# A small vision network on one core: norms and routing at both ends of the attention heads are moved amid neighbouring work

## The chip, the core and the metric

The kernel runs on one NeuronCore of a Trainium2 chip. The time is the device time of one execution in microseconds (us). Five engines run side by side, each through its own list of instructions, and wait for one another by semaphores: TensorE (PE: matrix products, into the eight banks of PSUM), VectorE (DVE), ScalarE (ACT: functions by table), GpSimd (POOL) and SyncE (SP: it issues transfers). "PEld" is TensorE's loading of stationary operands.

## What is computed

Four images of 224 by 224 with 3 channels are cut into 784 patches each, of 8 by 8 pixels. The steps, with h as the running state (784 tokens of 64 features per image):

```python
h = tokenizer(x)                              # two layer norms, a projection, a silu layer
h = h + gated_group_norm(layernorm(h))        # the sequence mixer; its group norm has groups of one
h = h + experts0(layernorm(h))                # shared MLP + 4 experts of 3 layers, top 2 (relu)
h = h + attention(layernorm(h))               # 8 heads, rank 32: softmax(q k / 8) x VO
h = h + experts1(layernorm(h))                # softmax router, top 2 of 8 experts: gelu(x w1 + b1) w2 + b2
```

A layer norm here is the mean taken off, then a product with (variance + 1e-5)^-0.5. The output holds h three times per image. What matters for the change: the norm before the attention can be taken image by image, since it needs the first expert layer of that image alone; the norm and the router before the last expert layer need all 8 heads of that image alone.

## The kernel before

**Layout.** An image's 784 tokens lie in two halves of 392 columns: rows 0 to 63 of a tile hold the features of the first half, rows 64 to 127 those of the second. `H` is the state, `xhat` the normalised state. P is the PSUM, `bank(n)` is 392 columns of bank n.

**A norm** (`norm(S)`, one in each engine's list; S is `ATT` before the attention and `MOE1` before the last expert layer) has these steps for images 0 to 3 together: TensorE centres `H` by a product into a bank; ScalarE squares it; VectorE copies it to `xhat`; TensorE averages the squares of all images into one bank, 32 rows per image; ScalarE loads the table of Ln, takes Ln, loads the table of Exp and takes Exp(-0.5 times that); TensorE spreads the result over 128 rows per image; VectorE multiplies it into `xhat` (semaphore `normed`).

**The first expert layer** is a loop over images b in all lists: second layer, shared second layer, then the first layer of image b+1, the gates broadcast by products, and the sums into bank 7, which VectorE adds to `H` (L1382, semaphore `h_ready`). ScalarE empties the hidden banks 0 to 3 (L535). Afterwards comes `norm(ATT)` for all four images.

**Projections.** `project_pair(b, n)` makes half of the heads' q or k of image b (n counts `QK_ORDER`: q and k of heads 0 to 3, q and k of heads 4 to 7). Each has to be split in a high and a low part (`QKH`, `QKL`). For image 0 ScalarE writes the high part and VectorE the low one (L568, L1390); for the others ScalarE writes the raw value (`project_raw`, L577) and GpSimd splits it (L676, L678; `qk_split` counts). SyncE copies the parts of a head into the stacks `Qs` and `Ks` with six transfers (`fill_stacks`, L389), sends features for the values (`features_in`, L379), values (`fill_values`, L393 and L394) and the row of negative maxima (`rows_to_stack`, L400), in one queue in the order of its list. Before the heads comes the lead-in, a loop over `LEAD` = 14 steps j: two products (`max_half`) whose row maxima VectorE takes (L1395), for heads 0 and 1; in between, by the table `BETWEEN`, projections and the values (`turn_values`) of later images. In the kernel before image 0 and image 1 are projected ahead of the lead-in and images 2 and 3 within.

**Heads.** `four_heads(i)` runs 4 heads; 8 calls make 32 heads, the middle six in a loop. A head is 14 score products (`score_half`), each exponentiated by ScalarE (L610), beside them the row-max products of the head two ahead, and then its context (`context_tile`, seven pairs), which ScalarE copies (L618, `CT`) and TensorE projects in the next head (`head_out`); VectorE divides (`divide`), GpSimd adds (`add_head`). The last two heads have no head two ahead, and so no row-max products.

**The end.** Then `OUT` is turned back onto `H` for all images ("join"), `norm(MOE1)` follows, the router's logits are turned, VectorE finds top 2 and gates (`route`, some 18 small instructions), TensorE turns the gates to rows and VectorE copies them (`wT1`). 16 steps m (image m // 4, expert pair m % 4) follow: a hidden layer, Gelu (L642), a broadcast of the gates, VectorE's product of both (L1525) and the second layer's product. Twelve hidden layers run ahead of the first gates. The sum of an image is added (L1517), turned, copied by ScalarE (L656) and stored, 3 copies for each of two parts, 21 of the 24 stores by SyncE and the last 3 by ScalarE (L363).

## Time and profile before

| | us |
|---|---|
| median of 3 runs | 611.97 |
| lowest and highest | 611.2, 613.12 |
| the profiled execution | 613.25 |
| its span in the profile | 611.4 |
| TensorE busy | 563.2 (92%) |
| VectorE busy | 373.6 (61%) |
| ScalarE busy | 328.4 (54%) |
| GpSimd busy | 75.2 (12%) |

The profile is of one execution. Its time is longer than its span by what lies before the first and after the last instruction. Matmuls are pipelined, so a busy TensorE isn't TensorE at its peak. A product of 4-byte numbers is two matmul instructions in it, a product of operands rounded for speed ("fp32r") is one.

### The profile page before, as it was taken

To read this page: it belongs to the slowest core of one execution; us is meant where nothing else is said; L and a number is where in the kernel's file an instruction comes from. 1 tells how busy PE (TensorE), PEld (TensorE's weight loads), DVE (VectorE), ACT (ScalarE), POOL (GpSimd) and SP (SyncE) were. 2 spreads that over 40 slices of the span, in tenths; PEclk is the share of its full clock that TensorE was granted. 3 is DMA by queue.
4 is the path that set the end of the run, shared out by engine and by line. 5 is a ranking of instruction groups with operands and counts; after the bars stand their busy time and mean duration, and the time that the engine had idled before them with its cause. 6 is when DMAs were issued, how large, how long until landed. Compare 5 with 4: busy or idle time off the path is not lost.

```text
span 611.4 us, 10204 instructions
## 1 busy us (share of the span) xinstructions
PE 563.2 (92%) x3076; PEld 330.1 (54%) x3076; DVE 373.6 (61%) x881; ACT 328.4 (54%) x726; POOL 75.2 (12%) x89
## 2 busy tenths in 40 slices
PE   0689799997989999999999999999999999997994
PEld 0454344443556566566576576666666676452441
DVE  3844754214697667677677577577577677036562
ACT  0464758563746456466466465465465565536521
POOL 0000000000696100100100100100100001112000
PEclk9999999998989999999999999999999999999997
DMA  6500000000551322322322422323323320000015
GB/s 171 227 0 2 0 0 2 0 1 14 125 144 40 102 72 66 99 68 73 93 64 75 97 58 78 94 58 82 90 58 88 84 58 19 2 1 1 1 39 119
DMA packets 21986, 37.65 MB, mean 62 GB/s; under 512 B 5560, under 2 KB 15224, under 8 KB 21704
## 3 DMA queue, kind: packets, MB, share of 16 engines
q1 hardware_dynamic: 21606, 36.82, 23.3%
q10 hardware_dynamic: 354, 0.50, 0.4%
q8 instruction: 14, 0.23, 0.2%
q14 instruction: 12, 0.10, 0.1%
HBM read 6.07 MB, written 2.41 MB: 14 GB/s over the span
## 4 chain that ended last, share of the span: by engine, by line
PE 89%; ACT 4%; DVE 2%; DMA 2%; issue 1%; SPq 0%; DVEq 0%
PE P L702 86%; DMA X<-x 2%; PE P L718 2%; PE P L985 1%; ACT L504 1%; ACT PT L610 1%; ACT g L642 1%; DVE bst L1187 1%; PE P L1125 0%; DVE xhat L1259 0%; SPq L369 0%; ACT act L513 0%; PE P L844 0%; PE P L955 0%; DVE mx L1395 0%
## 5 line engine op out<-in xcount | busy, mean ns | idle before, releaser
L1395 DVE TENSOR_REDUCE mx<-P 112x1 f32<-112x392 f32 x448 | 219.0, 557 | 96.2 <-PE P L702 91.8
L610 ACT ACTIVATE PT<-P 112x392 f32<-112x392 f32 x448 | 188.2, 494 | 26.6 <-PE P L702 25.5
L702 PE MATMUL P<-Ks,Qs 96*112 96x392 f32 x448 | 167.8, 379 | 1.0 <-DVE mx L1395 0.9
L702 PE MATMUL P<-Qs,Ks 98*112 98x392 f32 x448 | 155.3, 351 | 0.8 <-ACT PT L610 0.7
L702 PE MATMUL P<-PT,XVs 112*64 112x392 f32 x896 | 154.5, 496 | 0.0
L702 PEld LDWEIGHTS P<-PT,XVs 112*64 112x64 f32 x896 | 61.6, 137 | 79.3 <-issue 73.6
L702 PEld LDWEIGHTS P<-Ks,Qs 96*112 96x112 f32 x448 | 78.8, 178 | 42.7 <-issue 19.7
L618 ACT ACTIVATE CT<-P 128x392 f32<-128x392 f32 x32 | 15.9, 497 | 134.4 <-PE P L702 134.4
L702 PEld LDWEIGHTS P<-Qs,Ks 98*112 98x112 f32 x448 | 79.9, 179 | 6.2 <-ACT PT L610 3.7
L688 POOL TENSOR_TENSOR OUT<-OUT,part 120x448 f32<-120x448 f32 x27 | 30.7, 1136 | 274.1 <-DVE part L1422 274.1
L702 PE MATMUL P<-VBs,CT 128*112 128x130 f32 (+1 forms) x320 | 40.0, 261 | 0.6 <-ACT CT L618 0.6
L702 PE MATMUL P<-xhat,wa 64*128 64x392 f32 (+2 forms) x144 | 37.8, 560 | 1.4 <-DVE xhat L1259 1.4
L702 PEld LDWEIGHTS P<-VBs,CT 128*112 128x112 f32 (+1 forms) x320 | 35.3, 157 | 6.0 <-ACT CT L618 1.3
L535 ACT ACTIVATE h<-P,wa 128x392 f32<-128x392 f32 x48 | 24.5, 596 | 13.9 <-PE P L702 13.8
L718 PE MATMUL P<-wa,xn 112*96 112x112 f32 x56 | 12.1, 398 | 16.2 <-DVE xn L1200 16.2
L702 PEld LDWEIGHTS P<-xhat,wa 64*128 64x128 f32 (+2 forms) x144 | 17.1, 192 | 17.5 <-DVE xhat L1259 4.2
L676 POOL CAST QKH<-QKL 128x392 fp32r<-128x392 f32 x24 | 12.2, 507 | 110.9 <-ACT QKL L577 110.9
L678 POOL TENSOR_TENSOR QKL<-QKL,QKH 128x392 fp32r<-128x392 f32 x24 | 24.4, 1017 | 1.9
L1376 DVE TENSOR_TENSOR h<-P,h 128x392 f32<-128x392 f32 x16 | 8.3, 561 | 25.3 <-PE P L702 25.3
L1525 DVE TENSOR_TENSOR g<-P,g 128x784 f32<-128x784 f32 x16 | 15.5, 974 | 9.1 <-PE P L702 9.1
L1422 DVE TENSOR_TENSOR part<-P,zi 120x448 f32<-120x448 f32 x32 | 20.0, 625 | 1.6
L1415 DVE RECIPROCAL zi<-P 120x7 f32<-120x7 f32 x32 | 6.4, 201 | 23.6 <-PE P L702 23.6
(180 smaller groups left out, 466.3 us busy)
## 6 DMA issues: line engine op xcount, KB each, us to landing
Qs<-QKH SPq DMA_DIRECT2D x64, 98.0 KB, 2.2
Ks<-QKH SPq DMA_DIRECT2D x64, 98.0 KB, 2.2
XVs<-XV SPq DMA_DIRECT2D x32, 196.0 KB, 2.5
Qs<-QKL SPq DMA_DIRECT2D x32, 98.0 KB, 2.1
Ks<-QKL SPq DMA_DIRECT2D x32, 98.0 KB, 2.1
X<-x SPq DMA_DIRECT2D x4, 588.0 KB
wa<-table_a SPq DMA_DIRECT2D x1, 2207.5 KB, 8.3
VBs<-VB SPq DMA_DIRECT2D x32, 65.0 KB, 2.2
```

What stands on the lines that cost most here:

```text
L535: nc.scalar.activation(dst, P[0:rows, k % 4, 0:width], func, **({} if bias is None else dict(bias=bias)))\
L610: nc.scalar.activation(PT[:, u, c * HALF:(c + 1) * HALF], P[0:T, SCORE_BANK + half_in_loop(s, u, c) % RING, 0:HALF], ACT.Exp, scale=float( ...
L618: nc.scalar.activation(CT[:, :], bank(6), ACT.Copy).then_inc(ctx_done, 1)
L676: nc.gpsimd.tensor_copy(QKH[cols], QKL[cols].bitcast(F32)).then_inc(pool_hi, 1)
L678: nc.gpsimd.tensor_tensor(QKL[cols], QKL[cols].bitcast(F32), QKH[cols].bitcast(F32), ALU.subtract)\
L688: nc.gpsimd.tensor_tensor(OUT[:, b, :], OUT[:, b, :], part[:, h % HG % 3, :], ALU.add).then_inc(added, 1)
L702: return nc.tensor.matmul(dst, lhsT, rhs, start=start, stop=stop, **more)
L718: last = nc.tensor.transpose(P[0:KF, 2 * p + k, q * T:(q + 1) * T], xn[:, p, q, k * KF:(k + 1) * KF], A("ident", T)[:, 0:T])
L1376: nc.vector.tensor_tensor(buf, bank(WBC_BANKS[n % 2]), buf, ALU.mult).then_inc(wbc_done, 1)
L1395: nc.vector.tensor_reduce(mx[:, s % 2, c, t:t + 1], bank(n)[0:T, :], AX.X, ALU.max)\
L1422: nc.vector.tensor_tensor(part[:, s % 3, :].rearrange("p (t d) -> p t d", d=D), got[:, :, 0:D], zi[:, :].unsqueeze(2).broadcast_to([OROWS, ...
L1525: nc.vector.tensor_tensor(g1[:, b, p, :, :], P[:, n:n + 2, 0:HALF], g1[:, b, p, :, :], ALU.mult).then_inc(gate_used, 1)
```

## The change

Front: image 0's part of `norm(ATT)` runs within the first expert layer (its centring in the turn b = 1, its variance amid the first layer of image 2, its spreading in the turn b = 2; ScalarE's two tables, Ln and Exp at the end of its turn b = 2; VectorE squares this image itself). Image 1 is centred in turn b = 3. Image 0's q and k of heads 0 to 3 are projected before the last sums. After the layer only images 1 to 3 are normed (the variances of all four are taken again in one group), and image 0's other two projections go to GpSimd for splitting, which now has 28 of them, not 24. Image 1's four projections move into the lead-in. SyncE waits for q and k of the first stack one after the other, and all features of images 1 to 3 come after the second stack.

Back: images 0 to 2 are joined, centred and squared in the last head but one, normed, routed and turned in the last head. ScalarE takes their Ln and Exp before it copies that head's context. VectorE routes them before the last division. Image 3 alone is joined, centred and its variance taken between hidden layers 0 to 5; its Ln and Exp come after six Gelus, its spread, router, routing and gate rows in the steps 2, 4, 6, 7 to 9 and 10. Six hidden layers run ahead and not twelve; the others share one pair of banks, one per step. The gates use one pair of banks until step 10. Image 0's output is turned in steps 8 and 9, image 1's in 10 and 11, image 2's in 14 and 15.

```diff
-        BETWEEN = {0: ("qk", 2, 0), 1: ("qk", 2, 1), 2: ("qk", 2, 2), 3: ("qk", 2, 3), 4: ("xv", 1), 5: ("qk", 3, 0),
-                   6: ("qk", 3, 1), 7: ("qk", 3, 2), 9: ("qk", 3, 3), 10: ("xv", 2), 11: ("xv", 3)}
+        BETWEEN = {0: (("qk", 1, 0),), 1: (("qk", 1, 1),), 2: (("qk", 1, 2),), 3: (("qk", 1, 3),), 4: (("qk", 2, 0),),
+                   5: (("xv", 1), ("qk", 2, 1)), 6: (("qk", 2, 2),), 7: (("qk", 2, 3),), 9: (("qk", 3, 0),),
+                   10: (("xv", 2), ("qk", 3, 1)), 11: (("qk", 3, 2),), 12: (("qk", 3, 3),), 13: (("xv", 3),)}
+        RAW = [(b, n) for b in range(B) for n in range(4) if b or n >= 2]
...
+        AHEAD = 6
+        TANH_AT = 15
...
             def hidden_pair(m):
-            return 2 * (m % 2) if m < 3 * PAIRS else 0
+            return 2 * (m % 2) if m < AHEAD else 0
+        def gate_pair(m):
+            return 0 if m > AHEAD + PAIRS and m % 2 else 2
...
 SyncE
-            sync.wait_ge(qk_lo, 4)
-            fill_stacks(0, 0)
-            features_in(1)
+            fill_stacks(0, 0, queries=2, keys=4)
             fill_stacks(0, 1)
-            features_in(2)
-            features_in(3)
+            for b in range(1, B):
+                features_in(b)
...
 ScalarE, in the first expert layer, after image b's first layer
+                if b == 2:
+                    nc.scalar.preload_act_table_set(LN)
+                    scalar.wait_ge(var_full, ATT + 1)
+                    rstd(rs[0:R, :], P[0:R, 4, 0:HALF], eps[0:R, :])
-            norm(ATT)
...
+            nc.scalar.preload_act_table_set(LN)
+            for n in range(2):
                 project_high(n)
+            for b in range(1, B):
+                scalar.wait_ge(centred, 4 * (ATT - GATE) + b + 1)
+                nc.scalar.activation(sq[:, b, :], bank(3 + b), ACT.Square).then_inc(squared, 1)
+            scalar.wait_ge(var_full, ATT + 2)
+            rstd(rs[:, :], bank(7), eps[:, :])
+            for n in range(2, 4):
+                project_raw(0, n)
             values_out(0)
...
 ScalarE, in four_heads, before context_out
+                    if final and s == 2:
+                        for b in EARLY:
+                            scalar.wait_ge(centred, 4 * (MOE1 - GATE) + b + 1)
+                            nc.scalar.activation(sqm[:, b, :], bank(b), ACT.Square).then_inc(squared, 1)
+                        nc.scalar.preload_act_table_set(LN)
+                        scalar.wait_ge(var_full, FIRST_ROUND)
+                        rstd(rsm[0:LAST * R, :], P[0:LAST * R, 0, 0:HALF], eps[0:LAST * R, :])
+                    if final and s == 3:
+                        half_distance(0)
...
 ScalarE, the Gelus
-            for m in range(TANH_AT):
+            for m in range(AHEAD):
                 gelu(m)
+            nc.scalar.preload_act_table_set(LN)
+            scalar.wait_ge(var_full, FIRST_ROUND + 1)
+            rstd(rsm[0:R, :], P[0:R, LAST_BANK, 0:HALF], eps[0:R, :])
+            nc.scalar.preload_act_table_set("gelu_and_others")
+            for m in range(AHEAD, TANH_AT):
+                gelu(m)
...
+            half_distance(1)
+            rows_out_of(0, 0)
+            gelu(TANH_AT)
+            rows_out_of(0, 1)
...
 TensorE, in the first expert layer
+            def rows_amid(b):
+                rows_of(b)
+                if b == 1:
+                    variances((0,), 4)
...
+                if b == 2:
+                    spread_rstd((0,), ATT + 1)
+                elif b >= 1:
+                    centre(b // 2)
...
+                if b == B - 1:
+                    for n in range(2):
+                        project_pair(0, n)
...
-            norm(ATT, h_ready, lambda b: B + b + 1)
+            centre(2)
+            centre(3)
+            variances(range(B), 7)
+            for n in range(2, 4):
+                project_pair(0, n)
+            spread_rstd(range(1, B), ATT + 2)
...
 TensorE, in four_heads
+                        if final and s == 2 and u in (0, 2, 4):
+                            join(u // 2, u // 2)
+                        if final and s == 3:
+                            if u == 0:
+                                spread_rows(EARLY, 0)
+                            elif u == 2:
+                                router(EARLY, 0)
+                            elif u == 4:
+                                turn_router(EARLY, 1)
...
+                    if final and s == 2:
+                        for b in EARLY:
+                            centre_rows(b, b)
                     for u in range(NT):
                         context_tile(i, s, u, first and s == 0)
+                        if final and s == 2 and u == 2:
+                            row_variances(EARLY, 0)
...
 TensorE, the end
-            norm(MOE1, h_ready, lambda b: 2 * B + b + 1)
...
+            hidden_layer(0)
+            for half in range(2):
+                head_out(7, 3, False, half)
+            hidden_layer(1)
+            pe.wait_ge(gates_ready, 2)
+            pe.wait_ge(sel1_ready, 2)
+            rows_of_image(0)
+            pe.wait_ge(ctx_done, NH)
+            rows_of_image(1)
+            join(LAST, LAST_BANK)
+            pe.wait_ge(turned_done, 1)
+            rows_of_image(2)
+            hidden_layer(2)
+            centre_rows(LAST, LAST_BANK)
+            hidden_layer(3)
+            hidden_layer(4)
+            row_variances((LAST,), LAST_BANK)
+            hidden_layer(5)
             gate_of(0)
...
+                    if AHEAD + m < B * PAIRS:
+                        hidden_layer(AHEAD + m)
+                    if m == 2:
+                        spread_rows((LAST,), LAST_BANK)
+                    elif m == 4:
+                        router((LAST,), LAST_BANK)
+                    elif m == 6:
+                        turn_router((LAST,), LAST_BANK)
+                    elif m == 10:
+                        pe.wait_ge(gates_ready, 3)
+                        rows_of_image(LAST)
+                    if m in (8, 9):
+                        turn_out(0, m - 8)
...
 VectorE, the end
+            for stage in range(3):
+                route(EARLY, 1, stage)
             divide(7, 3)
...
+                if m == 3:
+                    normalised(LAST, LAST_BANK)
+                elif m == 5:
+                    copy_router((LAST,), LAST_BANK)
+                elif m in (7, 8, 9):
+                    route((LAST,), LAST_BANK, m - 7)
+                elif m == 10:
+                    rows_in(LAST)
```

## Rows read from the trace of the kernel before

**Rows 1.** The page's chain that ended last, its shares by engine.
```profile
PE 89%; ACT 4%; DVE 2%; DMA 2%; issue 1%; SPq 0%; DVEq 0%
```

**Rows 2.** Stretches: length, busy us of PE, PEld, DVE, ACT, POOL, clock, DMA, GB/s.
```profile
543.00:560.80 17.80, 14.45 (x119) 7.60 (x119) 9.37 (x19) 8.15 (x12) 5.33 (x5) 1.00 0.01 1
```

**Rows 3.** Stretches of 1 us; the granted clock is the first number after POOL's.
```profile
147.00:148.00 1.00, 0.00 (x0) 0.00 (x0) 0.00 (x0) 0.95 (x2) 0.00 (x0) 0.82 0.00 0
...
153.00:154.00 1.00, 1.00 (x4) 0.73 (x4) 0.73 (x3) 0.58 (x3) 0.00 (x0) 0.50 0.00 0
154.00:155.00 1.00, 1.00 (x5) 0.53 (x4) 0.99 (x2) 0.51 (x2) 0.00 (x0) 0.77 0.00 0
...
178.00:179.00 1.00, 0.39 (x2) 0.26 (x2) 1.00 (x3) 0.00 (x0) 1.00 (x2) 0.68 0.50 145
...
553.00:554.00 1.00, 0.00 (x0) 0.00 (x0) 0.10 (x1) 1.00 (x1) 0.00 (x0) 1.00 0.00 0
```

**Rows 4.** Timeline, 110 to 150: start, us, engine, line, what, [idle before, releaser].
```profile
110.88 1.54 ACT L535 ACTIVATE s<-P,wa 128x392 f32<-128x392 f32 x3
...
121.06 2.02 ACT L535 ACTIVATE h<-P,wa 128x392 f32<-128x392 f32 x4 [4.18 <-PE P L702]
...
141.16 2.90 PE L702 MATMUL P<-H,wb 128*128 128x392 f32 x8
141.27 0.63 DVE L1382 SCALAR_TENSOR_TENSOR H<-P,wa,H 128x392 f32<-128x392 f32 x1 [0.96 <-PE P L702]
...
145.53 0.59 ACT L503 ACTIVATE rs<-P,eps 128x392 f32<-128x392 f32 x1 [0.94 <-PE P L702]
146.14 1.28 ACT L504 ACT_TABLE_LOAD   x1
...
148.01 1.69 PE L702 MATMUL P<-rs,spread 32*128 32x392 f32 x8 [2.52 <-ACT rs L506]
```

**Rows 5.** Timeline, 155 to 180: first stack, lead-in, first score.
```profile
155.02 1.24 SPq L389 DMA_DIRECT2D Qs<-QKH  x2
...
160.75 0.62 PE L702 MATMUL P<-Ks,Qs 96*112 96x392 f32 x2
...
162.15 0.61 PE L702 MATMUL P<-Ks,Qs 96*112 96x392 f32 x2
...
162.69 0.93 PE L702 MATMUL P<-xhat,wa 64*128 64x392 f32 x4
...
166.91 0.60 PE L955 MATMUL P<-wb,XF 64*112 64x64 f32 x7
...
179.20 0.53 PE L702 MATMUL P<-Qs,Ks 98*112 98x392 f32 x1
```

**Rows 6.** Timeline, 532 to 548: copies of context, a context, the joins.
```profile
532.12 0.50 ACT L618 ACTIVATE CT<-P 128x392 f32<-128x392 f32 x1 [4.12 <-PE P L702]
...
537.70 4.83 PE L702 MATMUL P<-PT,XVs 112*64 112x392 f32 x28
...
542.58 0.50 ACT L618 ACTIVATE CT<-P 128x392 f32<-128x392 f32 x1 [4.12 <-PE P L702]
...
544.13 3.94 PE L702 MATMUL P<-wb,OUT 112*64 112x112 f32 x64
```

**Rows 7.** Timeline, 560 to 611: routing, steps, stores.
```profile
560.90 0.42 DVE L1475 COPY gate_p<-P 98x256 f32<-98x256 f32 x1 [1.53 <-PE P L829]
...
575.61 0.62 PE L702 MATMUL P<-wT,sel1r 96*128 96x392 f32 x2
...
577.83 0.62 PE L702 MATMUL P<-wT,sel1r 96*128 96x392 f32 x2
...
588.65 20.67 SPq L363 DMA_DIRECT2D out<-OT  x21
...
601.38 2.60 SPq L363 DMA_DIRECT2D out<-OT  x3
...
601.68 0.57 DVE L1517 TENSOR_TENSOR Y<-P,HX 128x392 f32<-128x392 f32 x1 [1.47 <-PE P L702]
```

More of the change, by code:

```diff
@@ L489, in _, with rstd @@
             tokens_out(6, 0)
+            def rstd(dst, variance, small):
+                nc.scalar.activation(dst, variance, ACT.Ln, bias=small).then_inc(act_step, steps.one())
+                nc.scalar.preload_act_table_set(EXP)
+                scalar.wait_ge(act_step, steps.now())
+                nc.scalar.activation(dst, dst, ACT.Exp, scale=-0.5).then_inc(rstd_ready, 1)
             def norm(S):
@@ L633, in _ @@
             four_heads(7, final=True)
-            norm(MOE1)
             nc.scalar.preload_act_table_set("gelu_and_others")
@@ L1028, in head_out, with join @@
                     last.then_inc(proj_full, 1)
+            def join(b, n):
+                if b in EARLY:
+                    pe.wait_ge(max_done, HEAD_HALVES * NH)
+                    pe.wait_ge(added, HEADS * (b + 1))
+                else:
+                    pe.wait_ge(summed, 1)
+                for k in range(HALF // T):
+                    for h in range(2):
+                        mm(P[h * D:(h + 1) * D, n, k * T:(k + 1) * T], OUT[0:T, b, (2 * k + h) * D:(2 * k + h + 1) * D],
+                           Bt("ident", T)[:, 0:T])
+                for h in range(2):
+                    own = slice(h * D, h * D + REST)
+                    last = mm(P[h * D:(h + 1) * D, n, HALF - REST:HALF], OUT[own, b, (NT - 1) * D:NT * D], Bt("ident")[own, own])
+                last.then_inc(join_full, 1)
@@ new lines, in centre_rows, with row_variances @@
+            def centre_rows(b, n):
+                pe.wait_ge(h_ready, 2 * B + b + 1)
+                mm(bank(n), Bt("center"), H[:, b, :]).then_inc(centred, 1)
+            def row_variances(images, n):
+                for b in images:
+                    pe.wait_ge(squared, B * MOE1 + b + 1)
+                    pe.wait_ge(copied, B * (MOE1 - POOL3) + b + 1)
+                    at = 0 if b == LAST else b * R
+                    last = mm(P[at:at + R, n, 0:HALF], means[:, :], sqm[:, b, :])
+                last.then_inc(var_full, 1)
@@ new lines, in spread_rows, with router @@
+            def spread_rows(images, n):
+                pe.wait_ge(rstd_ready, FIRST_ROUND + (LAST in images))
+                for b in images:
+                    rows = slice(0, R) if b == LAST else slice(b * R, (b + 1) * R)
+                    mm(bank(n + b % B if b != LAST else n), spread[rows, :], rsm[rows, :]).then_inc(rstd_full, 1)
+            def router(images, n):
+                for b in images:
+                    pe.wait_ge(normed, 4 * MOE1 + b + 1)
+                    at = 0 if b == LAST else b * R
+                    last = mm(P[at:at + R, n, 0:HALF], Bt("router"), xhat[:, b, :])
+                last.then_inc(logits_full, 1)
@@ L1030, in four_heads, with turn_router @@
+            def turn_router(images, n):
+                rows = len(images) * R
+                pe.wait_ge(logits_out, 2 + (LAST in images))
+                for ct in range(NGT):
+                    last = nc.tensor.transpose(P[0:GT, n, ct * rows:(ct + 1) * rows], gate1.lt[0:rows, ct * GT:(ct + 1) * GT],
+                                               Bt("ident", rows)[:, 0:rows])
+                last.then_inc(logits_turned, 1)
             def four_heads(i, first=False, final=False):
```

393 lines of the change are left out of this document (227 added, 166 removed).

## The prediction

> **What bounds the kernel now.** Three views, in this order. The chain of waits by engine: TensorE carries 89% of the span [rows 1], so a change pays only where TensorE stands still, runs at its lower clock, or where something beside it ends last. The busy time by stretch finds those places. The 29 heads between the two ends are the same instructions before and after. Of the 17.8 us after the last head TensorE is busy 14.45 [rows 2]. In the front the clock granted to TensorE falls within 147 to 148 us, after TensorE had stood from about 145.5, is 0.50 (1.2 of 2.4 GHz) up to 154, and rises within 154 to 155; it falls again within 178 to 179, after a patchy stretch, but not at 553 to 554, where TensorE stands as long [rows 3]. The timeline then gives the order of each serial chain.
>
> Front chain now: the expert layer's last sum ends, image 3's add on VectorE starts at 141.27; then centre, square, variance (Ln starts 145.53), table load, Exp, spread (148.01 to 149.70 at 1.2 GHz) [rows 4]; then image 0's four projections, their splitting, and only at 155.02 SyncE starts to fill the first stack. The lead-in (14 steps of two row-max matmuls) starts 5.73 later, at 160.75, lasts 18.45, and the first score is at 179.20 [rows 5]. Back chain now: last context copy at 542.58, joins, norm, routing (on VectorE from 560.90, some 18 instructions of up to 0.42), gates, and SyncE's 21 stores, 588.65 to 609.32, as the last thing issued [rows 6, 7].
>
> **The change, front.**
> Step 1, image 0's norm amid the expert layer: two centrings, a variance and a spread, four matmuls. Four centrings take 2.90 [rows 4], 0.73 each, so 0 to 2.9 us. They stand where ScalarE sets the pace (3 of its outputs in 1.54, back to back), so most is hidden; I take 0.9. The 3.7 us of ScalarE's two table loads, Ln and Exp (1.28+0.59+1.28, and 0.55 from the load's end at 147.42 to TensorE's answer at 148.01) fit its 4.18 us of idling before 121.06 [rows 4]; without that cover they would cost up to 3.7.
> Step 2, two projections of image 0 before the last sums: a projection's two halves take 0.86 (0.93 with the last one's drain) [rows 5], 1.75 for both, less some 0.5 in which TensorE waited for VectorE's products: 1.2. The add of image 3 starts at 141.27+0.9+1.2 = 143.4.
> Step 3, the first stack: it now waits for the add (0.63) and two splits, which no row here shows alone (bounds 0.2 and 0.63 each; I take 0.52, about what an add costs): SyncE starts at 145.1 instead of 155.02, its six transfers stay, and the lead-in can start 5.73 later, at 150.8. The norm of images 1 to 3 runs beside it: add, centre, square, variance to 146.1, Ln, load, Exp (2.4) to 148.5, during which TensorE does two more projections (1.75); spread, mean matmul and transposes end at about 150.7. Both arrive together, so a loss in either counts. TensorE's standing of 2.52 us [rows 4] shrinks to under 1, and I expect no fall of the clock there.
> Step 4, the lead-in: the upfront projections of image 1 (4) move into it, now 12 steps with one projection where there were 8. A step with one takes 1.40 (160.75 to 162.15), and an image's seven transposes about 0.6 more [rows 5]: 12x1.40 + 2x0.6 + 1.35 (step 8 with its turn) + 1.25 (the last) + 0.75 (wait for the last value copy) = 21.35. VectorE's 28 maxima, under 16 us, hide. First score at 150.8+21.35 = 172.15, against 179.20: **-7.0 us**. SyncE: 6 issues for the features, 12 for two more stacks and 2 for the values stand before the row of maxima; from 148.9 with 18 more in front of the first row it is past them near 165, before 172. GpSimd gets four more splits of 1.5 us but starts 6.5 us earlier, and ends where it did. The first head is held by VectorE's maxima, so the higher clock there is counted at nothing (0 to 3.3 more, half of the low 6.5 us).
>
> **The change, back.**
> Step 5, the last but one head: three joins (four take 3.94 [rows 6], so 0.97 each) enter a score phase of 5.6 us (10.46 per head less 4.83 for its context), in which TensorE has 4.2 of work; it becomes 7.1. Then three centrings, 2.0 to 2.2, and three variances, 0.9. This head ends 4.4 later than now, 536.5. ScalarE does three squares, load, Ln, load, Exp ahead of that head's copy and ends at about 536.1, barely in time: the cover is 0.4, and all beyond it is paid.
> Step 6, the last head: spread 0.7, router 0.8 and a wait of 0.7 for the normalised rows, turning 0.6: ends at 548.0 instead of 542.5. VectorE's routing of three images (18 instructions, each with three quarters of the elements of the 0.42 us one [rows 7], 0.37 with its own wait) starts at 543.7, runs beside the last context and ends at 550.5.
> Step 7, the join of the last image waits behind that routing: summed at 552.1. Hidden layers 0 to 5 are spread around it and end at 558.3; their Gelus end at 559.3. Then ScalarE must load Ln, load Exp, load Gelu again: 1.28x3+0.59+0.55 = 5.0, so Gelu 6 starts at 564.3, and TensorE, which could go on at 563.7, waits 1.6. From there an iteration with a hidden layer takes 2.22 (575.61 to 577.83) [rows 7], and ten remain where before four did. With image 3's spread, router, turning and gate rows (2.3 in all), the outputs' turning and some 0.5 of waits for VectorE's second routing, the last sum ends at about 598.5 to 599 instead of 601.6: -2.7 to -3.2.
> Step 8, the stores: image 0's block is turned at step 9 and copied at about 588.4, no earlier than now (588.65). 21 stores at 0.88 (three in 2.6 [rows 7]) then run without a gap, 588.6 + 18.5 = 607.1 against 609.3: **-2.3 us**, the least of the gains counts. Bounds: every us by which the ten iterations slip is lost here one for one (ends +2 and -3.5).
>
> A rule of the Trainium skill speaks against steps 5 and 7. The row: Ln starts 145.53 and lasts 0.59, the table load follows at 146.14 for 1.28, and TensorE has Exp's result at 148.01 [rows 4], so nothing lies between load and Exp. The page "ScalarE: Activation LUTs", in "What ACT_TABLE_LOAD costs", adds a drain of some 1.38 us to each switch, 2.66 in all. By the row the five switches added are 1.28 each; by the page two of them at step 5 and three at step 7 would weigh 2.7 and 4.1 us more. The trace disagrees, and I go by the row.
>
> **Sum**, against the profiled execution: 613.25, with a span of 611.4 and 1.85 around it; the median of the runs shown is 1.28 lower, 611.97. -7.0 - 2.3 = -9.3, which gives 604.0 for such an execution and **602.7** for a median.
>
> **Rivals.**
> A. The back gives nothing: ScalarE is late at step 5 or VectorE's queue holds up the join and the gates at step 7, by 2.3 us in all. For it: a cover of only 0.4 and seven queued rows of small instructions; against: the tail of stores had gaps to lose. -7.0: 605.0.
> B. The front gives half: the four matmuls of step 1 cost their 2.9 and ScalarE's table loads are not covered (another 1.5). For it: TensorE reads busy throughout; against: that is pipelined time. -3.5-2.3: 606.2.
> C. Slower: the clock. Each fall lasted some 6.5 us and cost half, 3.3. The new order has short waits at about 150, 538, 552, 559 and 564. If the clock falls at all five, 16.5 are paid: 619. It decides from three falls on, where the gain is used up. For it: the fall at 178 to 179 came with no long pause; against: at 553 it did not fall, and after 568 TensorE is full.
> D. By the skill's rule above as a mechanism: each switch stalls ScalarE 1.38 more, late by 2.7-0.4 at step 5 and 4.1 at step 7, 6.4 in all: 609.1.
> E. The reordering doesn't do what it says, since the first score still waits for the row of maxima behind SyncE's issues: then the front gives 1 or 2, 608.5.
>
> **How the numbers follow.** Forecast (599 to 604.9) 0.55, A 0.16, B 0.12, C 0.07 (0.02 of it within 0.3% of before, where three falls just use up the gain, 0.05 beyond), D 0.03, E 0.05, and 0.02 for a loss that I do not see. A measurement of this kernel can tell about 0.3%, 1.8 us, from no change. Slower is 0.05+0.02 = 0.07, same 0.02, faster the rest, 0.91. The range is 599.0 to 608.0: it takes in A and B and the lower ends of steps 1 and 8, and leaves out C, D, most of E and the unseen loss, about 0.17.
>
> **What would show it.** Right: first score at 171 to 174; lead-in starting at 150 to 152 and lasting 21 to 22; no 0.50 clock between 147 and 172; last context copy 32 heads later at about 541 (548 less 7); six Gelus, then about 5 us of ScalarE without one; 21 stores without a gap. Wrong: a first SyncE issue for a stack later than 147; a fall of the clock in the last 60 us; stores with gaps before image 2's.

## The result and the profile after

| | before | after |
|---|---|---|
| median, same chip (us) | 611.59 (4 runs, 610.97 to 613.12) | 605.65 (4 runs, 603.89 to 606.41) |
| the profiled execution | 613.25 | 605.98 |
| its span | 611.4 | 604.2 |
| TensorE, VectorE, ScalarE, GpSimd busy | 563.2, 373.6, 328.4, 75.2 | 561.1, 376.7, 337.7, 81.6 |

The ratio is 0.989, with a 95% interval of 0.987 to 0.991. A second set of the same kernel gave 0.987 (0.986 to 0.989). Predicted were 602.7 and a range of 599 to 608: the direction and the main mechanism hold; the gain is 6 us in this set and 8 in the second, where 9.3 were forecast. The ratios leave out three executions that lie over 1.5% above the fastest of their kernel: 622.94 and 1327.12 of the kernel with extra products, 615.34 of the one without table switch.

The page's chain of the kernel after, by engine. TensorE's share is one point higher than in [rows 1], and nothing else has grown much:

```profile
PE 90%; DVE 3%; ACT 3%; DMA 2%; issue 1%; SPq 0%; DVEq 0%
```

Stretches of the kernel after (length, busy us and count of PE, PEld, DVE, ACT, POOL, then clock, DMA share, GB/s). First one from 541.30, 1.6 before the last context's copy, to 560.50, just behind the start of the seventh hidden layer; it answers to [rows 2]. Then stretches of 1 us in which the clock changed or had changed before, against [rows 3]:

```profile
541.30:560.50 19.20, 15.88 (x95) 7.50 (x92) 10.66 (x23) 13.04 (x15) 0.00 (x0) 1.00 0.00 0
...
62.00:63.00 1.00, 0.52 (x4) 0.52 (x8) 0.95 (x3) 0.98 (x2) 0.00 (x0) 0.73 0.00 0
69.00:70.00 1.00, 1.00 (x4) 0.50 (x2) 0.68 (x2) 1.00 (x3) 0.00 (x0) 0.86 0.00 0
147.00:148.00 1.00, 1.00 (x8) 0.14 (x2) 1.00 (x3) 0.43 (x1) 0.00 (x0) 1.00 0.00 0
175.00:176.00 1.00, 1.00 (x6) 0.85 (x5) 1.00 (x4) 0.46 (x2) 0.92 (x2) 0.55 0.09 16
178.00:179.00 1.00, 1.00 (x6) 0.96 (x5) 0.92 (x3) 0.75 (x3) 0.92 (x2) 0.74 0.01 3
```

The fall at 147 is gone; TensorE is busy all through that microsecond. The one at the first head is 3.5 us long instead of 7. And there is one at 62 to 69, in a part of the kernel that the change doesn't touch. All twelve executions profiled later, three of them with the front of before, have a fall between 61 and 70 too, 3 to 7 us long; the profiled execution of before is the only one without. Image 0's add comes 0.98 late (109.70 instead of 108.72). Of this, 0.87 is lost in the stretch with the fall: the table loads at 62.45 and 84.56 lie 22.11 apart, before those at 62.35 and 83.59 lay 21.24 apart. That is chance and not the change: over the fourteen profiled executions the add lies anywhere from 107.38 to 109.70, and the same kernel after, profiled once more with the same fall, has it at 108.71.

Timeline of the kernel after, the front. It answers to [rows 4, 5]:

```profile
109.70 0.63 DVE L1562 SCALAR_TENSOR_TENSOR H<-P,wa,H 128x392 f32<-128x392 f32 x1 [1.94 <-PE P L775]
...
119.12 1.28 ACT L599 ACT_TABLE_LOAD   x1
...
122.81 0.62 DVE L1562 SCALAR_TENSOR_TENSOR H<-P,wa,H 128x392 f32<-128x392 f32 x1 [1.93 <-PE P L775]
...
145.29 0.62 DVE L1562 SCALAR_TENSOR_TENSOR H<-P,wa,H 128x392 f32<-128x392 f32 x1 [2.14 <-PE P L775]
...
146.89 1.24 SPq L419 DMA_DIRECT2D Qs<-QKH  x2
...
148.37 0.59 ACT L527 ACTIVATE rs<-P,eps 128x392 f32<-128x392 f32 x1 [0.94 <-PE P L775]
148.97 1.28 ACT L528 ACT_TABLE_LOAD   x1
...
150.27 0.53 ACT L530 ACTIVATE rs<-rs 128x392 f32<-128x392 f32 x1
...
150.85 0.94 PE L775 MATMUL P<-rs,spread 32*128 32x392 f32 x6 [1.00 <-ACT rs L530]
...
152.67 0.60 PE L1072 MATMUL P<-wb,XF 64*112 64x64 f32 x7
153.20 0.60 PE L775 MATMUL P<-Ks,Qs 96*112 96x392 f32 x2
...
154.59 0.60 PE L775 MATMUL P<-Ks,Qs 96*112 96x392 f32 x2
...
173.74 0.34 PE L775 MATMUL P<-Qs,Ks 98*112 98x392 f32 x1
```

TensorE's wait ahead of the spread is 1.00 (2.52 in [rows 4]); the six matmuls of the spread take 0.94 (eight took 1.69 at the low clock, and 0.94 at the high one in the kernel with the longer lead-in alone, below). The first score comes 5.46 earlier.

Timeline of the kernel after, the last two heads (against [rows 6]):

```profile
515.11 0.50 ACT L663 ACTIVATE CT<-P 128x392 f32<-128x392 f32 x1 [4.19 <-PE P L775]
...
522.88 2.14 PE L775 MATMUL P<-H,wb 128*128 128x392 f32 x6
...
527.07 0.86 PE L775 MATMUL P<-sqm,means 128*32 128x392 f32 x6
...
530.64 0.93 PE L775 MATMUL P<-rsm,spread 32*128 32x392 f32 x6
530.76 0.50 ACT L663 ACTIVATE CT<-P 128x392 f32<-128x392 f32 x1 [0.35 <-PE P L775]
...
542.94 0.50 ACT L663 ACTIVATE CT<-P 128x392 f32<-128x392 f32 x1 [1.62 <-PE P L775]
```

And its end (against [rows 7]): the block of table loads, the line of stores, the last sum.

```profile
554.07 1.28 ACT L706 ACT_TABLE_LOAD   x1
...
555.36 0.58 ACT L527 ACTIVATE rsm<-P,eps 32x392 f32<-32x392 f32 x1
...
555.96 1.28 ACT L528 ACT_TABLE_LOAD   x1
...
557.25 0.53 ACT L530 ACTIVATE rsm<-rsm 32x392 f32<-32x392 f32 x1
...
557.80 1.28 ACT L709 ACT_TABLE_LOAD   x1
...
559.10 0.91 ACT L701 ACTIVATE g<-P,wb 128x784 f32<-128x784 f32 x1
...
560.06 0.93 PE L775 MATMUL P<-xhat,wb 64*128 64x392 f32 x4 [1.35 <-ACT g L701]
...
583.37 18.66 SPq L393 DMA_DIRECT2D out<-OT  x21
...
593.30 0.56 DVE L1752 TENSOR_TENSOR Y<-P,HX 128x392 f32<-128x392 f32 x1 [1.47 <-PE P L775]
...
595.57 3.23 ACTq L393 DMA_DIRECT2D out<-OT  x3
```

SyncE's line ends at 602.03, 8.7 after the last sum's add; before it ended 7.6 after it (609.32 and 601.68). The last part of the kernel is a line of stores and no computation. The span ends another 2.2 us behind this line (2.1 before).

**Where the 7.27 went.** Measured from mark to mark in the two profiled executions: up to image 0's add +0.98 (the clock, by chance); from there to the first copy of a context 83.70 before and 76.24 after, -7.46; the heads between, -0.08; from the 30th copy of a context (521.67; 515.11) to the end of SyncE's line 87.65 and 86.92, -0.73. The front gave what was forecast, the back a third of it.

Part of the front's 7.46 is clock: the fall at 147 cost 1.9 (shown below by the kernel with extra products), and from the first score to the first context copy it is 12.20 instead of 13.22, as the fall there is shorter. By these two numbers 2.9 is clock and 4.6 the new order. The shorter falls go with the new front. None of its ten profiled executions has a fall at 147, and the one in the first head is 3.5 us long in eight and absent in two. Of the four with the old front two have a fall at 147, and three have one of 7 us at the first head.

### The profile page after: what moved, and what is told of

Its sections match the earlier page's. It is cut to its first block, busy times and chain, and to the rows that moved or that the text cites. A ratio compares the mean times of both kernels' runs of the same rounds, so it can differ in the third digit from the quotient of the medians.

```text
span 604.2 us, 10259 instructions
## 1 busy us (share of the span) xinstructions
PE 561.1 (93%) x3082; PEld 327.0 (54%) x3082; DVE 376.7 (62%) x899; ACT 337.7 (56%) x734; POOL 81.6 (14%) x97
## 4 chain that ended last, share of the span: by engine, by line
PE 90%; DVE 3%; ACT 3%; DMA 2%; issue 1%; SPq 0%; DVEq 0%
PE P L775 86%; DMA X<-x 2%; PE P L791 2%; ACT L528 1%; DVE mx L1590 1%; PE P L1089 1%; PE P L1283 1%; DVE bst L1367 1%; SPq L399 0%; ACT PT L655 0%; ACT g L701 0%; PE P L917 0%; DVE xhat L1439 0%; PE P L1072 0%; DVE xn L1380 0%
## 5 line engine op out<-in xcount | busy, mean ns | idle before, releaser
L775 PE MATMUL P<-xhat,wa 64*128 64x392 f32 (+2 forms) x144 | 35.1, 530 | 0.7 <-DVE xhat L1439 0.7
L743 POOL TENSOR_TENSOR QKL<-QKL,QKH 128x392 fp32r<-128x392 f32 x28 | 28.6, 1021 | 2.2
L741 POOL CAST QKH<-QKL 128x392 fp32r<-128x392 f32 x28 | 14.3, 510 | 105.1 <-ACT QKL L617 105.1
L701 ACT ACTIVATE g<-P,wb 128x784 f32<-128x784 f32 x16 | 14.5, 914 | 18.1 <-PE P L775 18.0
L775 PEld LDWEIGHTS P<-xhat,wa 64*128 64x128 f32 (+2 forms) x144 | 14.4, 181 | 14.4 <-issue 3.7
```

The costliest lines, as they stand in the source:

```text
L701: nc.scalar.activation(g1[:, m // PAIRS, m % PAIRS, :, :], P[:, n:n + 2, 0:HALF], ACT.Gelu, bias=Bt("mb1")[:, m % PAIRS:m % PAIRS + 1]).th ...
L741: nc.gpsimd.tensor_copy(QKH[cols], QKL[cols].bitcast(F32)).then_inc(pool_hi, 1)
L743: nc.gpsimd.tensor_tensor(QKL[cols], QKL[cols].bitcast(F32), QKH[cols].bitcast(F32), ALU.subtract)\
L775: return nc.tensor.matmul(dst, lhsT, rhs, start=start, stop=stop, **more)
```

## The experiments

All ratios are to the kernel before on the same chip. Marks: T0 is image 0's add, T30 the 30th copy of a context. Times from mark to mark are those of the profiled executions.

**The front alone.** The change without its back half (six Gelus ahead, norm and routing in the heads are as before):

```diff
-        AHEAD = 6
+        GATE_PAIRS = (4, 2)
...
+            norm(MOE1)
...
-            for m in range(AHEAD):
+            for m in range(TANH_AT):
```

> Only the front half of the change (image 0's norm amid the first expert layer, its first two projections before the last sums, image 1's projections in the lead-in); the end is as before. My theory: the front carries nearly all of the gain, the first score at about 173.7 of the trace against 179.2 and the first context copy 6.5 us earlier, so this kernel takes 6.5 us less than before (605). Rival 1: the front and the back share the gain as the prediction had it, 7.0 and 2.3. Rival 2: the 6.5 us are partly given back at the end, since the stores of SyncE then wait for nothing: less than 5 us.

607.37 (604.18 to 607.89), ratio 0.990 (0.988 to 0.992): -5.6, for the theory's -6.5. T0 to the first copy of a context is 76.18, as in the whole change. The front alone carries nearly all of the gain. The clock fell at 549 to 554 in the profiled execution, and its stores start 68.15 after T30 instead of 66.98.

**The back alone.** The same cut from the other side:

```diff
-        FIRST_RING = ((0, 1), (2, 3))
+        FIRST_RING = ((4, 5), (6, 7))
...
-                if b == 2:
-                    nc.scalar.preload_act_table_set(LN)
-                    scalar.wait_ge(var_full, ATT + 1)
-                    rstd(rs[0:R, :], P[0:R, 4, 0:HALF], eps[0:R, :])
+            norm(ATT)
```

> Only the back half (images 0 to 2 joined, normed and routed beside the last two heads, image 3 among the hidden layers); the front is as before. My theory, from the trace of the changed kernel, where the last context copy but two is 6.56 us earlier and the last store 7.29: the back gives 0.7 us, 0 to 1.5. Rival (the prediction's step 8): 2.3 us.

611.05 (609.86 to 613.7), ratio 0.998 (0.996 to 0.999): -1.9, with an interval from -2.5 to -0.6. T30 to the end of SyncE's line is 86.70, 0.95 less than before. The trace stands nearer to the 0.7 of the theory, the median nearer to the 2.3 of the rival, and the interval allows both. -5.6 and -1.9 add up to -7.5, against -5.9 and -7.9 for the two sets of the whole: no interaction that these runs can tell.

**Stores split.** The whole change, with the second stores of images 1 and 2 issued by GpSimd:

```diff
-                for j in range(OJ if b < B - 1 else 1):
+                for j in range(OJ if b == 0 else 1):
                     store(sync, b, j)
...
             base(LAST)
+            store(pool, 1, 1, stored_pool)
+            store(pool, 2, 1, stored_pool)
```

> The changed kernel with 6 of SyncE's 21 stores (one half of image 1 and of image 2) issued by GpSimd. Theory A: the end is bound by SyncE's issuing, 21 stores at 0.89 us in one row from the first finished block on. Then the last issue comes when ScalarE's last three do, at about 598.5 instead of 602.0 of the trace: 3 us less than the changed kernel, so 602.5. Theory B: the end is bound by the transfers themselves, which share the same engines: no change, 605.6. Between: GpSimd issues slower than SyncE and ends last, 604.

602.55 (601.07 to 605.26), ratio 0.984 (0.981 to 0.986). In a second set 603.07, ratio 0.985 (0.983 to 0.988). Its median is 2.5 below the change's on the same chip (605.05), where theory A said 3 and theory B nothing; the intervals of the two ratios just touch. Part of it may be clock, since its executions had a mean granted clock of 0.984 to 0.995 against 0.974 to 0.985. Timeline of its end, and one stretch of it:

```profile
581.71 15.33 SPq L394 DMA_DIRECT2D out<-OT  x15
...
585.47 1.87 POOL L394 DMA_DIRECT2D out<-OT  x3 [21.29 <-ACT OT L719]
...
591.60 1.73 POOL L394 DMA_DIRECT2D out<-OT  x3 [4.26 <-ACT OT L719]
...
593.92 3.25 ACTq L394 DMA_DIRECT2D out<-OT  x3
```

```profile
597.00:598.00 1.00, 0.00 (x0) 0.00 (x0) 0.00 (x0) 0.00 (x0) 0.00 (x0) 0.50 0.87 194
```

SyncE ends at 597.04 and ScalarE, behind the last output, at 597.17: now both ends are even, and from T30 it is 83.72 to the last issue instead of 86.92. But not all of these 3.2 arrive. The span ends 3.3 us behind the last issue here and 2.2 behind it in the change, so that from T30 to the end of the span it is 87.05 instead of 89.09: 2.0. The stores' transfers themselves keep the 16 DMA engines busy 0.81 to 0.87 of the time from 596 to 599, so theory B's limit may be near; no run shows whether they set this end.

**The same kernel after, again.**

```diff
 (no edit)
```

> The changed kernel once more, as the measure for the other three. In the profiled execution of the changed kernel the clock of TensorE fell at 62 to 69 us, ahead of anything that the change touches, and cost 0.98 us there. If that is chance, this profile need not have it, its span is near 603.2 and the median 605 (gain 6.5 with an interval of some 1 us). If it belongs to the changed kernel (another layout in memory), it is there again, at the same place.

605.05 (604.55 to 606.22). From T0 to the first copy of a context 75.54, from T30 to the end of the stores 87.05. The clock also fell at 554 to 558 here, and not in the first head, the opposite of the first profiled execution: where it falls is not fixed by the kernel. The fall at 62 is there again, but it is in kernels with the front of before too, so it doesn't belong to the change.

**The longer lead-in alone.** The kernel before, with image 1's four projections moved into the lead-in, and nothing else:

```diff
-        BETWEEN = {0: ("qk", 2, 0), 1: ("qk", 2, 1), ...
+        BETWEEN = {0: (("qk", 1, 0),), 1: (("qk", 1, 1),), ...
...
-            for n in range(4):
-                project_pair(1, n)
```

> The kernel before with one edit: image 1's four projections moved from ahead of the lead-in into it (the table BETWEEN of the changed kernel). Theory: the lead-in starts when the first stack has landed, whatever TensorE does before it, so the start stays at 160.7 of the trace and only the length grows, from 18.45 to some 20.5 us: 2 us slower than before. Rival: the projections ahead of the lead-in are what delays it, and the move alone brings 1 us or more.

618.96 (613.07 to 620.97), ratio 1.011 (1.007 to 1.015): 6.7 slower, where the theory said 2. Its timeline and a stretch:

```profile
148.61 0.94 PE L700 MATMUL P<-rs,spread 32*128 32x392 f32 x8 [2.52 <-ACT rs L507]
...
155.98 0.99 PE L700 MATMUL P<-XV,wb 112*120 112x455 f32 x2 [1.28 <-DVE QKL L1385]
...
159.16 0.99 PE L700 MATMUL P<-Ks,Qs 96*112 96x392 f32 x2 [1.65 <-DMA Ks<-QKH]
...
161.69 0.67 PE L700 MATMUL P<-Ks,Qs 96*112 96x392 f32 x1
```

```profile
157.00:171.00 14.00, 12.36 (x35) 5.13 (x37) 5.16 (x10) 4.08 (x9) 8.17 (x12) 0.53 0.69 157
```

The projections of image 1 had been what TensorE did while the first stack was filled. Without them it stands, 1.28 and 1.65, the clock falls within 157 to 158 and stays low through 14 us in which TensorE is busy 12.36 of them, and a step takes 2.53 instead of 1.40. Even without that fall nothing would be gained. The lead-in starts 17.30 after image 3's add (19.48 before), but 1.9 of these 2.2 are there because the clock didn't fall at 147 in this execution: from the add to SyncE's first issue it is 11.89, as in the kernel with extra products (next), whose lead-in starts 17.40 after the add. The move itself gives 0.1 and makes the lead-in 2.1 longer (20.54 in the kernel after, 18.45 before): the theory's 2 us, and the low clock on top. What pays in the front is that SyncE's first issue comes earlier, and that the norm fills the time in which the stack is filled.

**Products in the norm's gap.** The kernel before, with three extra products, results not used, while ScalarE loads tables:

```diff
-            norm(ATT, h_ready, lambda b: B + b + 1)
+            def keep_warm(b):
+                if b < 3:
+                    mm(bank(5 + b % 2), Bt("ident"), H[:, 0, :])
+
+            norm(ATT, h_ready, lambda b: B + b + 1, meanwhile=keep_warm)
```

> The kernel before with three idle products (0.73 us each, results never read) in the 2.5 us in which TensorE waits for the inverse root before the attention. Theory: the fall of the clock at 147.8 comes from that wait. With it gone the chain from the spread to the first stack runs at 2.4 GHz, the first SyncE issue for a stack comes 2 us earlier than 155.02 and the kernel takes 1.5 to 2.5 us less than before; then that much of the front's 7.5 us is the clock and the rest the order. Rival: the fall hardly counts, since ScalarE and VectorE set the pace there: less than 0.5.

613.47 (before 612.24 on this chip), ratio 1.002 (1.000 to 1.004): the theory's 1.5 to 2.5 us less didn't come. Two of its microseconds:

```profile
147.00:148.00 1.00, 0.77 (x8) 0.31 (x8) 0.00 (x0) 0.17 (x1) 0.00 (x0) 1.00 0.00 0
...
553.00:554.00 1.00, 1.00 (x8) 0.20 (x8) 0.00 (x0) 1.00 (x1) 0.00 (x0) 0.68 0.00 0
```

There is no fall at 147, and from image 3's add to SyncE's first issue it is 11.89 instead of 13.75, so that fall was worth 1.9. That the products took it away isn't shown: the kernel with the longer lead-in alone has the whole wait of 2.52 [148.61 above] and no fall there either. And the 1.9 doesn't last. At the first context copy only 1.1 of it is left, since the fall in the first head now lies wholly within it (14.13 from the first score to the copy, 13.22 before). In this execution the clock also fell at 553 to 561, where before's had not, and the stores start 69.19 after T30 instead of 66.98.

**No table switch at the end.** The change without the three loads of step 7; image 3's inverse root isn't taken, its variance is copied:

```diff
-            nc.scalar.preload_act_table_set(LN)
             scalar.wait_ge(var_full, FIRST_ROUND + 1)
-            rstd(rsm[0:R, :], P[0:R, LAST_BANK, 0:HALF], eps[0:R, :])
-            nc.scalar.preload_act_table_set("gelu_and_others")
+            nc.scalar.activation(rsm[0:R, :], P[0:R, LAST_BANK, 0:HALF], ACT.Copy).then_inc(rstd_ready, 1)
```

> The changed kernel with image 3's inverse root at the end left out (ScalarE copies the variance with one instruction in place of Ln, Exp and three table loads). Theory: the waits of TensorE at 555.9 to 560.1 of the trace are ScalarE's 5.0 us without a Gelu; without them stores and end come 2.0 to 2.8 us earlier than in the changed kernel. Rival: the iteration is bound by VectorE's products and their one pair of banks, and under 1 us comes back.

604.13, ratio 0.988 (0.986 to 0.990), not to be told from the change. The stores start 66.84 after T30 instead of 68.26: the block of loads costs 1.42 here, between the theory's 2.0 and the rival's 1, and not the 5.0 that it lasts, since TensorE has work for the rest.

**One table for Ln and Exp.** ScalarE loads a set that holds both, in all norms, so a load between them falls away:

```diff
-        LN, EXP, SILU = "natural_log", "exp_and_others", "silu_and_others"
+        LN, EXP, SILU = "natural_log_exp_and_others", "exp_and_others", "silu_and_others"
...
                 nc.scalar.activation(dst, variance, ACT.Ln, bias=small).then_inc(act_step, steps.one())
-                nc.scalar.preload_act_table_set(EXP)
                 scalar.wait_ge(act_step, steps.now())
```

> The changed kernel with Ln and Exp of every norm taken from one table that holds both, so that no load stands between them; Exp's own table is loaded afterwards where it is needed. Seven inverse roots lose 1.28 us each between Ln and Exp. Theory: five stand alone on the chain (tokens, pool, gate, first experts, attention), image 0's and the two at the end are beside other work: 6.4 us less than the changed kernel, some 1 us more where TensorE's clock then doesn't fall at 62 us. Rival: the load is hidden behind something in most of them: 2 us. Ln of this table may be less exact.

607.26 (603.62 to 609.05), ratio 0.993 (0.990 to 0.995): by the medians some 2 us slower than the change, with intervals that just touch, though the profiled execution, 603.62, is faster than the change's. The theory's 6.4 us fell. In the first norms the load was covered. TensorE's products between variance and spread end last in three of four. In the other it is VectorE, as the timeline of this kernel shows (its last line is the start of the lead-in):

```profile
60.61 0.68 DVE L1462 COPY VB<-P 64x512 f32<-64x512 f32 x1 [1.29 <-PE P L776]
...
62.89 0.29 DVE L1411 TENSOR_TENSOR eb3r<-wa,eb3r 96x128 fp32r<-96x128 f32 x1
63.21 1.98 DVE L1440 TENSOR_TENSOR xhat<-xhat,P 128x392 f32<-128x392 f32 x4
...
151.39 0.61 PE L776 MATMUL P<-Ks,Qs 96*112 96x392 f32 x2 [0.35 <-ACT QKL L618]
```

The spread was ready at 61.7, 1.5 before VectorE came to it behind seven copies of operands that are needed much later. Ahead of the lead-in the load is gained (it starts 5.66 after SyncE's first issue, not 6.31), but the first score comes 26.96 after that issue instead of 26.85: the turning of the first maxima now waits 0.46 for VectorE. At the end the stores start 66.97 after T30 instead of 68.26. So 1.3 is gained at the end of this execution. Most of the others are 3 us and more above it, and they had less clock: 0.977 to 0.982 on average in the four from 606.80 to 609.05, against 0.988 and 0.990 in the two at 603.62 and 604.32. Where it fell in them, and whether the change of tables has to do with it, stays open.

**Front alone with split stores.** To see what the back half is worth once the stores don't end the kernel. The edits of the two experiments together.

```diff
-        AHEAD = 6
+        GATE_PAIRS = (4, 2)
...
+            store(pool, 1, 1, stored_pool)
+            store(pool, 2, 1, stored_pool)
```

> The front half of the change alone (routing and last norm as in the kernel before), with the second stores of images 1 and 2 issued by GpSimd (6 issues) so that SyncE has 15 left. It tells what the back half is worth once the line of stores no longer ends the kernel. Theory (the back half does shorten the computation by some 2 us, and the line of 21 stores hides most of it): here the last outputs of image 3 end the kernel, about 1.9 us before SyncE's line did, so 605.5 against front_only's 607.4, and stays about 2.5 to 3 us above the same split of the stores on the whole change. Rival (the back half is worth 0.7 us and no more, whatever the stores do): this kernel lands within 1 us of the whole change with split stores, about 603.

> The whole change with the same split of the stores as front_pool, a second time and on the same chip as it. Both theories: 602 to 603 as before; it is the yardstick for the three others of this set. SyncE's 15 stores start 68.3 after the 30th context copy.

Front with split stores 604.95, ratio 0.989 (0.986 to 0.991); whole change with split stores, in the same set, 603.07, ratio 0.985 (0.983 to 0.988). The back half is then worth 1.9 in the medians, 0.33% in the ratios, with intervals that overlap a little; the theory said 605.5 and 2.5 to 3 of distance, the rival 603 and under 1, so what was measured lies nearer to the theory. On the front alone the split takes 2.4 off the median (0.1% off the ratio, unclear), and from T30 to the end of the stores it is 86.60 instead of 88.82, both with a fall at 549 to 552. The end of the first kernel, and the clock in two microseconds of the second:

```profile
581.67 18.38 SPq L377 DMA_DIRECT2D out<-OT  x15
...
596.98 3.24 ACTq L377 DMA_DIRECT2D out<-OT  x3
```

```profile
555.00:556.00 1.00, 1.00 (x5) 0.30 (x4) 0.75 (x1) 0.99 (x2) 0.00 (x0) 0.82 0.00 0
556.00:557.00 1.00, 1.00 (x6) 0.29 (x4) 0.23 (x1) 0.98 (x2) 0.00 (x0) 0.50 0.00 0
```

In this execution of the whole change with split stores the clock fell at 555 to 563, and in the first set's it didn't. Its stores start 69.98 after T30, against 68.26 there. This fall of 7 us costs 1.7.

**Both tunings together.** Split stores and one table.

```diff
-        LN, EXP, SILU = "natural_log", "exp_and_others", "silu_and_others"
+        LN, EXP, SILU = "natural_log_exp_and_others", "exp_and_others", "silu_and_others"
...
+            store(pool, 1, 1, stored_pool)
+            store(pool, 2, 1, stored_pool)
```

> Split stores, and ScalarE's table set that holds both Ln and Exp in every norm. Theory 1 (only the load at step 7 and the one before the lead-in are ever waited for; in the four early norms TensorE's products or VectorE's queue of set-up copies end last): first add unchanged, the stores' start 67.0 instead of 68.3 after the 30th context copy, and since image 3's outputs end this kernel, 1.3 us less than the split stores alone, about 601.3. Rival (where TensorE's clock falls decides more than a load: the fewer waits only move its falls): no difference within 1 us, or worse by the 2 to 3 us by which the fuller norms alone came out slower.

605.77 (600.26 to 606.87), ratio 0.988 (0.985 to 0.992). The theory's 601.3 fell. In the median it is 2.7 worse than the split stores alone, as the rival has it, but the intervals overlap. One execution, 600.26, is the fastest of the whole study, the other five lie 3.9 to 6.6 above it; its mean granted clock was 0.992, theirs 0.970 to 0.986. The profiled one has a fall at 556 to 564, and its stores start 69.90 after T30, as with the two loads and the same fall (69.98). Without a fall one table gave 66.97, so here a fall of 7 us costs 2.9 and takes the table's gain with it.

**Products in step 7's gap.** Split stores and two extra products, results not used, before the seventh hidden layer:

```diff
+                    if m == 1:
+                        pe.wait_ge(turned_done, 2)
+                        for _ in range(2):
+                            mm(bank(6), Bt("ident"), H[:, 0, :])
                     if AHEAD + m < B * PAIRS:
                         hidden_layer(AHEAD + m)
```

> Split stores, and two extra products of TensorE (128x392, results not used) ahead of the seventh hidden layer of the last stage, where TensorE stands for 1.35 us on ScalarE's table loads. Theory (the fall of the clock at 554 to 557 seen in one execution is set off by these short waits, and costs 1 to 2 us where it comes): no 0.50 clock between 550 and 565 in the profile, and a median 0 to 1 us under the split stores alone. Rival (the fall comes of something else, and the two products delay the hidden layer by what they overhang, up to 0.4 us): same or up to 0.5 us slower, with or without a fall there.

603.3 (602.45 to 606.01), ratio 0.987 (0.984 to 0.989): no difference to 603.07. No fall between 550 and 565 in its profile, and the hidden layer starts 44.95 after T30, as without the products. But one profile without a fall proves little, as the split stores alone had one with and one without, and the median decides for neither theory.

## Why the prediction was right in sign and 3 us too good

The mechanism held and the sizes of some terms didn't. What failed is the overlap: work put beside other work was counted as mostly hidden (the four matmuls of step 1 at 0.9, three joins at 1.5), and it cost 1.87 and 2.1. In the back the joins and the work put into the last head made the stores start 1.5 us later than forecast, and since their line ends the kernel the back gave 0.73 instead of 2.3. Against the before of its own chip the second set misses the forecast gain by 1.4 us only, so part of the 3 us is the spread between sets.

**Steps 1 and 2, a size off.** Image 3's add was put at 143.4 and came at 145.29, 0.98 of it by the chance fall. A turn of the expert layer takes 13.11 and 13.20 where it took 12.35: step 1 costs 0.76+0.86+0.25 = 1.87, twice the 0.9 taken and within its bounds. "Most is hidden" in ScalarE's pace was wrong. The tables were covered as said: loads, Ln and Exp follow image 2's turn [119.12 above]. Step 2 cost 1.17, taken 1.2.

**Step 3, right in kind.** SyncE's first issue comes 1.60 after the add (taken 1.7). The lead-in starts 6.31 after it, not 5.73: TensorE's side was the later of the two, spread, mean product and transposes ending at 153.2, 7.91 after the add (taken 7.3). With one table less it is 5.66, and TensorE then waits 0.35 for ScalarE's raw values [151.39 above]; where the transfers end last, in the kernel with the longer lead-in alone, it is 5.41. So "both arrive together" was nearly right, and the loss came from TensorE's side. The fall at 147 is gone; it had cost 1.9, by the kernel with extra products.

**Step 4, right.** The lead-in lasts 20.54 for 21.35. Its steps are 1.40 as predicted; the transposes add 0.39 each and not 0.6, and steps 8 and 9 together take 2.33 for 2.75. From image 0's add to the first score 6.44 are gained, 7.05 forecast. The first head was counted at nothing and gave 1.0, since the clock was low for 3.5 us and not 7. So -7.46 for -7.0: the total is right, partly by luck, as an error of 0.6 and one of 1.0 nearly cancel.

**Steps 5 and 6, a size off, and the cause of the back's miss.** From T30 to the next two copies 14.9 and 26.3 were forecast, 15.65 and 27.83 measured. The pieces moved into the score phases of the last heads found less free time than the sum "5.6 less 4.2 of work" says. Three joins made 5.6 into 7.8 us up to the centrings (taken 7.1). ScalarE was in time, with a wait of 0.35 before the copy [530.76 above], so its cover of 0.4 held. Spread, router and turning cost the rest: the next head takes 12.18, not 11.5.

**Step 7, right.** From the last copy on nothing more was lost: T30 to the seventh hidden layer 44.95 (43.6 forecast), to the stores' start 68.26 (66.7), the same 1.4 to 1.6 late. The wait for Gelu 6 is 1.35 (1.6). Leaving the loads out gains 1.42.

**Step 8, right in kind.** It said that every us by which the iterations slip is lost one for one. They slipped 1.5, the 21 stores run without a gap at 0.889 each (0.88), and -2.3 (by its own numbers, 607.1 against 609.3, -2.2) became -0.73. By its own sum the last add was to come 2.7 to 3.2 earlier; it came 1.82 earlier from T30 (78.19; 80.01). The least of two gains counted; with the stores split, the kernels with and without the back half lie 1.9 apart.

**The rivals.** B came nearest for the time (a gain of 5.8, measured 5.9), but by luck: its front of -3.5 was -7.46, and of its mechanism only half is there, step 1 at 1.87 with the tables covered. A's back of nothing is near -0.73, by heads that are too long and not by ScalarE or VectorE being late. C is real but smaller: a fall between 549 and 564 came in some executions, one at a time. One of 7 us cost 1.7, 2.2 or 2.9 up to the stores' start and not 3.3, one of 3.5 us 0.1 to 1.2. D, the drain of the Trainium skill ("ScalarE: Activation LUTs", "What ACT_TABLE_LOAD costs"), is refuted here: 555.36+0.58 is 555.94 and the load starts at 555.96; 557.24 is its end and Exp starts at 557.25. No more than 0.02 lies beside 1.28. E didn't come: the products ahead of the first score wait 0.63 for ScalarE's last value copy. Of the signs, the first score (173.74), SyncE's first issue (146.89), the six Gelus with 5 us without one behind them and the 21 stores without a gap came as said. The lead-in started at 153.20 for 150 to 152 and took 20.54 for 21 to 22, and the sign against, a fall of the clock in the last 60 us while TensorE still worked, came in three of the eight profiled executions with the whole change.

## What to carry to other kernels

Before you value a shorter computation, look at what ends the kernel: where a line of transfers by one queue runs 7 to 9 us past the last sum, it takes most of the gain, and a second queue for six of its issues brought more (2.5 us in the medians, 2.0 in the profiled executions) than the rearranged end. Look behind the last issue too, as the transfers of a faster line can end later behind it. Work moved "beside" a phase bounded by something else costs part of its time even there: here 2.1 of the 2.9 us of three joins, and 1.9 of at most 2.9 for the centrings, variance and spread of image 0's norm. Take two thirds as paid, not a third or a half. And move work out of a gap only together with what fills the gap, since moving the projections alone made this kernel 1% slower.

## What the runs showed of the hardware

The clock granted to TensorE falls in different places in executions of one and the same kernel: at 554 to 558 in one profiled execution of the kernel after and nowhere there in the other. A wait of 2.52 before the spread was followed by a fall at 147 to 148 in two executions and by none in a third, the kernel with the longer lead-in alone. A fall of 7 us with TensorE busy cost 1.9 ahead of the first stack and 1.7, 2.2 and 2.9 ahead of the stores, each less than half of its length; a likely reason is that other engines pace part of the work there, which no run here isolates. Beside a lead-in bound by TensorE it is dear: 14 us at the low clock, steps of 2.53 for 1.40.

GpSimd issues three stores in 1.87 (0.62 each), SyncE one in 0.889 and ScalarE three in 3.23. No time beside the load's own 1.28 us shows around a table load: Ln, load and Exp follow within 0.02 [555.36 above].
